# Last three tiles of a routed expert stage added through one-hot products instead of a scatter, with adds on GpSimd and stores on SyncE

## The reference, cut to what matters

```python
x = x + L0_ffn(L0_cond(x))      # attention-like pooling, then 8 dense experts of 512, gated by a k-th value
x = x + L1_ffn(L1_cond(x))      # adapter and layer norm, then the routed experts below
# L1_ffn(x):
xn = layernorm(x) * gamma + beta
probs = softmax(xn @ gate_w)                 # 8 experts
w, idx = top_k(probs, 2); w = w / sum(w)     # two experts for each token
h = gelu(xn @ w1[e] + b1[e]); out_e = h @ w2[e] + b2[e]
output = sum over the two experts of w * out_e
return output + x
```

## Time and profile before

| what | us |
|---|---|
| median of 3 runs | 396.54 (393.29 to 401.63) |
| profiled execution, time | 395.97 |
| profiled execution, span | 394.1 |
| granted TensorE clock, mean over the span | 0.926 |

### The profile page before, as it was taken

How to read it: one execution, slowest core, us unless ns; L and a number is a source line. 1 busy time by engine, 2 the same in 40 slices (tenths; PEclk the granted TensorE clock), 3 DMA queues, 4 the chain that set the end, 5 groups by cost and what they waited for, 6 DMA issues and landing times.

```text
span 394.1 us, 9605 instructions
## 1 busy us (share of the span) xinstructions
PE 338.7 (86%) x3422; PEld 243.9 (62%) x3422; DVE 282.7 (72%) x779; ACT 250.0 (63%) x345; POOL 101.9 (26%) x97
## 2 busy tenths in 40 slices
PE   8999999888999999999979969699886934889930
PEld 5657776666777666767756646477664713567720
DVE  1746589999999978798977999735666422546684
ACT  3368588677998887998887758455653503346520
POOL 0000000000000000122227575404345372526770
PEclk9897999999999999999999989799986885999995
DMA  6993003022443674500001012211211012121354
GB/s 189 291 373 107 2 0 98 25 70 58 124 151 130 228 245 173 220 2 2 2 0 42 16 49 59 71 23 41 63 27 55 16 54 69 39 57 55 116 148 141
DMA packets 27059, 35.80 MB, mean 91 GB/s; under 512 B 6581, under 2 KB 22853, under 8 KB 26789
## 3 DMA queue, kind: packets, MB, share of 16 engines
q1 hardware_dynamic: 21600, 28.40, 23.1%
q0 software_dynamic: 2400, 4.95, 3.8%
q10 hardware_dynamic: 3012, 1.84, 1.5%
HBM read 29.18 MB, written 16.25 MB: 115 GB/s over the span
## 4 chain that ended last, share of the span: by engine, by line
PE 61%; DVE 16%; issue 8%; ACT 6%; another core or an unknown queue 5%; DMA 2%; POOL 1%; ACTq 0%; DVEq 0%; SPq 0%; POOLq 0%
PE bank L663 5%; DVE l L710 5%; PE psA L616 5%; PE psA L617 5%; PE psA L618 5%; PE bank L665 5%; PE bank L664 5%; PE bank L653 4%; PE psA L601 4%; PE psA L597 3%; PE psA L603 3%; PE psA L602 2%; PE bank L654 2%; PE bank L1068 2%
## 5 line engine op out<-in xcount | busy, mean ns | idle before, releaser
L710 DVE SCALAR_TENSOR_TENSOR l<-h 128x1024 f16<-128x1024 f32 (+1 forms) x90 | 104.7, 1165 | 15.3 <-ACT h L703 15.0
L663 PE MATMUL bank<-w,h 128*128 128x128 f16 x512 | 91.2, 221 | 3.4 <-issue 2.1
L689 ACT ACTIVATE h<-psA,b1f 128x512 f32<-128x512 f32 (+1 forms) x100 | 76.7, 800 | 25.6 <-PE psA L618 21.9
L703 ACT ACTIVATE h<-h 128x1024 f16<-128x1024 f32 (+1 forms) x90 | 91.0, 1011 | 1.4
L665 PE MATMUL bank<-w,l 128*128 128x128 f16 x512 | 91.2, 221 | 0.0
L664 PE MATMUL bank<-w,h 128*128 128x128 f16 x512 | 91.1, 221 | 0.0
L1816 POOL DMA_INDIRECT sorted_out<-w,xe x43 | 50.3, 1169 | 49.0 <-DVE w L1865 23.3
L684 ACT ACTIVATE h<-psA 128x1024 f32<-128x1024 f32 (+1 forms) x22 | 22.1, 1004 | 59.9 <-PE psA L603 42.6
L663 PEld LDWEIGHTS bank<-w,h 128*128 128x128 f16 x512 | 50.5, 99 | 13.9 <-issue 6.0
L1404 POOL TENSOR_SCALAR rs<-mv 128x4 f32<-128x4 f32 x8 | 4.0, 498 | 200.3 <-DVE mv L1385 199.9
L664 PEld LDWEIGHTS bank<-w,h 128*128 128x128 f16 x512 | 50.5, 99 | 5.6
(11 more groups left out here) (214 smaller groups left out, 574.3 us busy)
## 6 DMA issues: line engine op xcount, KB each, us to landing
sorted_in<-in_pad SPq DMA_DIRECT2D x14, 715.0 KB, 7.1
w<-in_w SPq DMA_DIRECT2D x8, 512.0 KB, 5.6
wraw<-in_w SPq DMA_DIRECT2D x8, 512.0 KB, 3.8
first<-sorted_in SPq DMA_DIRECT2D x43, 65.0 KB
w<-sorted_out SPq DMA_DIRECT2D x6, 256.0 KB, 3.9
mg<-in_maskt SPq DMA_DIRECT2D x8, 128.5 KB, 3.5
acc<-in_xtm SPq DMA_DIRECT2D x2, 512.0 KB, 5.5
mg<-in_gbc SPq DMA_DIRECT2D x8, 128.0 KB
```

Source lines behind the costliest of these rows:

```text
L663: pe.matmul(oo, a, w_h, start=(c == 0 and k == 0), stop=False, skip_group_check=True)
L689: last = act.activation(dst[:, q * w:q * w + w], src[:, q * w:q * w + w], ACT.Gelu_apprx_tanh, bias=b1f[:, es[q] * 4 + c:es[q] * 4 + c + 1 ...
L703: act.activation(wide(h16, h16_at[u], u), wide(h32, h32_at[u], u), ACT.Copy, scale=HS).then_inc(s_hi, 1)
L710: dve.scalar_tensor_tensor(wide(l16, h16_at[u], u), wide(h32, h32_at[u], u), HS, wide(h16, h16_at[u], u), ALU.mult, ALU.subtract).then_inc ...
```

## The change

It does six things.

- `HOTP = 2`: the last two pairs, tiles 40 to 42 (`HOT` = 3), are not scattered. For each of their rows the weight of its choice is computed on the spot: the row carries a third word, the difference of the two best router values (`ROW` = D + 3), ScalarE takes its tanh (`act_ht`), VectorE makes the weight (`dve_hw`) and then a 128x512 matrix with that weight where the row's token number equals the column's (`dve_hot`, against `iota`, the numbers of group 3's tokens). TensorE multiplies it with `yo` in fp32 (`pe_hot`, four products of 128x128x128 for a tile) and gathers all three tiles in one PSUM bank; VectorE adds it to group 3 in two halves (`add_hot`). As not every row of group 3 is now written in `sorted_out`, both its parts are zeroed early (`zero_rows`).
- `last_load` waits for tiles 0 to 39 alone.
- `POOL_GROUPS = (0,)`: group 0's results are weighed and added on GpSimd, in four operations on 128x512 (`pool_adds`). The adds of groups 1 and 2 stay on VectorE, in steps of two.
- The stores of groups 0 to 2 move from ScalarE's queue to SyncE's, behind SyncE's own `last_load`, in the order 2, 1, 0.
- The turned copies of pairs 13 to 21 move from VectorE to ScalarE.
- Many numbers of MID, PRO, AT, TILE, SPACE, BP, W0HI and W0LO are changed by small amounts.

```diff
-ROW = D + 2
+ROW = D + 3
+HOTP = 2
+POOL_GROUPS = (0,)
...
+HOT = 1 + 2 * (HOTP - 1) if TPB[-1] % 2 else 2 * HOTP
...
-TILE = [1.35, 1.26, 1.27]
+TILE = [1.35, 1.29, 1.28]
...
-     "top": 18, "tanh": 17.4, "wk": 29, "rk": 19.7, "rkd": 21.7, "sc": 21.7, "gd": 32, "gT": 35.8, "gTc": 35.4, "b2m": 35.8,
+     "acc": 15.6, "top": 18.4, "tanh": 17.4, "wk": 26.7, "rk": 20.1, "rkd": 20.7, "sc": 19.1, "gd": 31.2, "gT": 33.5,
...
-      "out": 3.2, "in": 9.3, "b2": 3.2, "moe0": 3.5, "moe1": 12.6, "moeg": 3.6, "moek": 1.8, "yg": -5.5, "ygs": 0.7,
-      "tab": 0.45}
+      "out": 3.2, "in": 9.3, "b2": 3.2, "moe0": 0.4, "moe1": 12.6, "moeg": 3.45, "moek": 1.6, "yg": -9, "ygs": 0.4,
+      "tab": 0.45, "hots": -5, "hot": 2.5, "pm": 3, "pms": 1.05}
...
+            if g == NG - 1:
+                terms.extend((MO[g] + AT["moek"] * h, "moe", (g, h)) for h in range(2))
+            elif g not in POOL_GROUPS:
+                terms.extend((MO[g] + AT["moeg"] * (g - len(POOL_GROUPS)) + AT["moek"] * (k + 0.5 * h), "moe", (g, k, h)) for k in range(2) for h in range(2))
+        for h in range(2):
+            terms.append((MO[NG - 1] - AT["moek"] + 0.5 * h, "hot", (NG - 1, h)))
...
+        def add_hot(i, v):
...
+                dve.wait_ge(t_hot, 1)
+                o = bank[mb[("hot", 0)][0]].rearrange("p (t d) -> p t d", t=4)[:, 2 * h:2 * h + 2, :]
+                a = acc[:, 4 * g + 2 * h:4 * g + 2 * h + 2, 0:D]
+                dve.tensor_tensor(a, a, o, ALU.add).then_inc(s_acc, 1)
...
+        def zero_rows(sp):
+            for k in range(2):
+                sp.dma_start(scy[k * N + N - 512:k * N + N, :], t["zero"]).then_inc(t_pad, 16)
...
-            at("pool", m2_pos(u, last) + AT["out"], pool_out)
+            if i < NTL - HOT:
+                at("pool", m2_pos(u, last) + AT["out"], pool_out)
...
+            def act_ht(act):
...
+                act.activation(hth[:, h0:h1].unsqueeze(2), xrf[:, tiles[0]:tiles[-1] + 1, D + 2:D + 3], ACT.Tanh, scale=0.5).then_inc(t_ht, 1)
...
+            def dve_hw(dve):
...
+                link(dve, "dve", dve.tensor_tensor(hw[:, h0:h1], hsg[:, h0:h1], hth[:, h0:h1], ALU.mult))
+                link(dve, "dve", dve.tensor_scalar(hw[:, h0:h1], hw[:, h0:h1], c, c, ALU.mult, ALU.add))
...
+            def dve_hot(i):
...
+                    dve.tensor_scalar(hots[:, j, :], iota, xrf[:, i, D + 1:D + 2], hw[:, j:j + 1], ALU.is_equal, ALU.mult)\
+                        .then_inc(t_hp, 1)
...
+            def pe_hot(pe):
+                o = misc_bank(pe, ("hot", 0))
+                pe.wait_ge(t_yo, n + 1)
+                pe.wait_ge(t_hp, h1)
+                for i in tiles:
+                    j = i - (NTL - HOT)
+                    for x in range(4):
+                        last = pe.matmul(o[:, x * 128:x * 128 + 128], hots[:, j, x * 128:x * 128 + 128], yo[:, yo_at(i), :],
+                                         start=(j == 0 and x == 0), stop=(j == HOT - 1 and x == 3), skip_group_check=True)
...
+            if n >= NP - HOTP:
+                p = m2_pos(US + n, len(tiles) - 1) + AT["y"]
+                at("act", mpos[("t", n)] + AT["tc"] + 0.1, act_ht)
+                at("dve", mpos[("t", n)] + AT["xe"] + 0.7, dve_hw)
+                for i in tiles:
+                    at("dve", p + AT["hots"] + 0.5 * (i - tiles[0]), dve_hot(i))
+                at("pe", p + AT["hot"], pe_hot)
...
-            if b < NB - 1:
-                at("act", mpos[("t", n)] + AT["tc"], act_x)
-            else:
-                at("dve", mpos[("t", n)] + AT["tc"], dve_x)
+            at("act", mpos[("t", n)] + AT["tc"], act_x)
...
-                scattered(eng, NTL)
+                scattered(eng, NTL - HOT)
...
+        def pool_adds(g, n):
...
+                w = wk[:, g, k, :].unsqueeze(2).to_broadcast([128, 4, D])
+                link(pool, "pool", pool.tensor_tensor(y, y, w, ALU.mult))
...
+                pool.tensor_tensor(group_acc(g), group_acc(g), y, ALU.add).then_inc(t_pm[g], 1)
...
-            at("act", 997 + 0.1 * g, store(g))
+            if g in POOL_GROUPS:
+                for n in range(4):
+                    at("pool", tpos(NTL - 1) + AT["pm"] + AT["pms"] * (4 * g + n), pool_adds(g, n))
+            at("sp", 998 + 0.1 * (NG - 1 - g), store(g))
         for h in range(2):
             q = ("sp", "act")[h]
-            at(q, 998 if h == 0 else 999, last_load(h))
+            at(q, 998, last_load(h))
             at(q, 1999, last_store(h))
```

More of the change, by code:

```diff
@@ L287, in build_adaln_ffn @@
         xa, x2, xn = (pro[:, n:n + 512].rearrange("p (t d) -> p t d", d=D) for n in (1024, 1536, 2048))
+        hots = pro[:, 0:HOT * 512].rearrange("p (t n) -> p t n", t=HOT)
+        iota = mg[:, 0:512]
         xsf = pro[:, 2560:2560 + 8 * ROW].rearrange("p (t d) -> p t d", t=8)
@@ L330, in build_adaln_ffn @@
         xk = sb("xk", [128, 2])
+        hsg, hth, hw = (sb(x, [128, HOT]) for x in ("hsg", "hth", "hw"))
         tei = sb("tei", [128, NB, 2, TPM], I32)
@@ L363, in build_adaln_ffn @@
         t_end = sem("t_end")
+        t_ht = sem("t_ht")
+        t_pm = [sem(f"t_pm{g}") for g in POOL_GROUPS]
+        t_hp = sem("t_hp")
+        t_hot = sem("t_hot")
         t_pad = sem("t_pad")
@@ L370, in build_adaln_ffn @@
         t_tr = sem("t_tr")
-        t_xt = [sem(f"t_xt{b}") for b in range(NB)]
+        t_xt = sem("t_xt")
         t_yo = sem("t_yo")
         t_so = [sem(f"t_so{i}") for i in range(NSO)]
-        t_yg = [sem(f"t_yg{i}") for i in range(NG * 2 + 2)]
+        t_yg = [sem(f"t_yg{i}") for i in range(NG + 1)]
         p_at = sem("p_at")
@@ L482, in group_of @@
         def group_of(kind, v):
-            return STEPS[v[1]][v[2]][1] if kind == "y" else (v[0] if kind == "moe" else v)
+            return STEPS[v[1]][v[2]][1] if kind == "y" else (v[0] if kind in ("moe", "hot") else v)
         b2_pos = [max(PG + 1.5 + KEPT * ND, 0) + 1.0 + AT["b2"] * g for g in range(NG)]
@@ L492, in build_adaln_ffn @@
             terms.append((mid_pos("b2x", g), "b2x", g))
-            for k in range(2):
-                terms.append((MO[g] + (AT["moeg"] * g if g < 3 else 0.0) + AT["moek"] * k, "moe", (g, k)))
+            if g == NG - 1:
[4 more added lines that the diff above has]
+            terms.append((MO[NG - 1] - AT["moek"] + 0.5 * h, "hot", (NG - 1, h)))
         terms.sort(key=lambda x: x[0])
@@ L521, in build_adaln_ffn @@
             misc.append((upos[US + n] - AT["t"], ("t", n), turned_at(n)))
+        misc.append((tpos(NTL - 1) + 3.0, ("hot", 0), None))
         misc.sort(key=lambda x: x[0])
@@ L742, in before @@
             g = group_of(terms[i][1], terms[i][2])
-            prior = [j for j in range(i) if group_of(terms[j][1], terms[j][2]) == g and terms[j][1:] != ("moe", (NG - 1, 0))]
+            other = [(k, (NG - 1, 1 - terms[i][2][1])) for k in ("moe", "hot")] if g == NG - 1 and terms[i][1] in ("moe", "hot") else []
+            prior = [j for j in range(i) if group_of(terms[j][1], terms[j][2]) == g and terms[j][1:] not in other]
             if prior:
@@ L810, in fn @@
                     return
-                for j in range(4):
+                for j in (2 * half, 2 * half + 1):
                     last = dve.scalar_tensor_tensor(acc_of(4 * g + j), yg[:, g, k, j, :], wk[:, g, k, j:j + 1],
@@ L815, in add_moe, with fn @@
             return fn
+        def add_hot(i, v):
+            g, h = v
+            def fn(dve):
+                before(dve, i)
+                dve.wait_ge(t_hot, 1)
+                o = bank[mb[("hot", 0)][0]].rearrange("p (t d) -> p t d", t=4)[:, 2 * h:2 * h + 2, :]
+                a = acc[:, 4 * g + 2 * h:4 * g + 2 * h + 2, 0:D]
+                dve.tensor_tensor(a, a, o, ALU.add).then_inc(s_acc, 1)
+            return fn
         for i, (pos, kind, v) in enumerate(terms):
-            make = {"y": gated, "b2": add_b2, "x2": add_x2, "b2x": add_b2x, "moe": add_moe}[kind]
+            make = {"hot": add_hot, "y": gated, "b2": add_b2, "x2": add_x2, "b2x": add_b2x, "moe": add_moe}[kind]
             at("dve", pos, make(i, v))
@@ L1878, in dve_xe @@
                                          xrf[:, i:i + k, D + 1:D + 2], ALU.mult, ALU.add).then_inc(t_xe, 1)
+                if n >= NP - HOTP:
+                    j = i - (NTL - HOT)
+                    link(dve, "dve", dve.tensor_scalar(hsg[:, j:j + k], xk[:, 0:k], 2.0, -1.0, ALU.mult, ALU.add))
+            h0 = tiles[0] - (NTL - HOT)
+            h1 = h0 + len(tiles)
+            def act_ht(act):
+                for i in tiles:
+                    act.wait_ge(t_xr[i % NX], 16 * (i // NX + 1))
+                act.activation(hth[:, h0:h1].unsqueeze(2), xrf[:, tiles[0]:tiles[-1] + 1, D + 2:D + 3], ACT.Tanh, scale=0.5).then_inc(t_ht, 1)
@@ new lines, in dve_hw, with fn @@
+            def dve_hw(dve):
+                c = 0.5 / (WS * HS)
+                dve.wait_ge(t_ht, n - (NP - HOTP) + 1)
+                link(dve, "dve", dve.tensor_tensor(hw[:, h0:h1], hsg[:, h0:h1], hth[:, h0:h1], ALU.mult))
```

(12 more changed lines are left out.)

59 lines of the change are left out of this document (41 added, 18 removed), and 46 rows, old and new, of tables (MID, PRO).

## The result

| what | before | after |
|---|---|---|
| median, same chip and session, 11 runs each | 394.90 us | 397.43 us |
| ratio to before, 95% interval | | 1.0092 [1.0046, 1.0137] |
| profiled execution, time | 395.97 | 397.19 |
| profiled execution, span | 394.1 | 395.4 |
| mean granted clock over the span | 0.926 | 0.929 |

The changed kernel is about 1% slower, where 393.5 was predicted against 396.54 (a ratio of 0.992). It lies inside the range given (up to 398.5), on the other side of no change.

What follows compares the result with a forecast made beforehand. TensorE's work bounds the last stage, a chain of handovers the end. Copies +0.7 and one-hots +0.95, then VectorE's 10.2 us list, end the span at 391.1 instead of 394.1: 393.5 us against the 396.54 median, range 387.5 to 398.5.

Steps and rivals of the forecast that it cites:

- So the next pair starts about 0.1 late, which eight pairs (14 to 21) make some 0.7: Last stage of tiles: turned copy behind ScalarE's activation delays each next pair about 0.1 us, some 0.7 in all.
- 8 × 0.47 = 3.8: Last stage: upper bound in us for the copies, if each of eight pairs pays ScalarE's full 0.47.
- fits in what TensorE still has to do: Pair 19: the one-hot's 0.4 us delay on VectorE is hidden under TensorE's remaining work, so costs nothing.
- rival C: Last stage: ScalarE's copy costs its full 0.47 per pair, 3.8 us instead of 0.7; time 396.6; chance 0.11.
- TensorE works at 100% there, which covers most of it: Last stage: argument against the copy costing its full 0.47 us per pair, as TensorE's full business hides most.
- A: End: rival that GpSimd's group 0 adds and VectorE's adds lock each other out, adding 2.2 us; time 395.7; chance 0.2.
- 20 adds beside scatters in 5.58: End: argument against the GpSimd lock, VectorE's adds beside GpSimd's scatters being no slower than 0.28 us each.
- 16.9 us were forecast: End: time from pair 20's activation to the span's end, with VectorE's list of 10.2 us as the bound.
- rival B: End: GpSimd's four ops at 2.6 us each finish last and delay SyncE's stores; time 400.9; chance 0.08.
- T + 4.4: Pair 20: its low part on VectorE ends 4.4 us after its activation starts, 0.95 later than before.
- The tables, costed at 0: Whole kernel: retiming by the moved positions was given no cost or gain, with a range of ±3 us.
- rival D: Before 328 us: moved positions shorten the 14.6 us hole, a third of it giving 4.9 us more; chance 0.18.

Runs made afterwards that it cites:

- e2: Changed kernel with group 0's adds back on VectorE instead of GpSimd, copies still on ScalarE: median 396.26 us, 1.0047 of before.
- e1: Changed kernel with the turned copies of pairs 13 to 21 back on VectorE, all else as changed: median 392.93 us, 0.9927 of before.
- e4: Kernel before with only the turned copies of pairs 13 to 21 moved to ScalarE: median 401.04 us, 1.0158 of before.
- e7: Changed kernel with copies and group 0's adds on VectorE and the old number tables except AT: median 375.29 us, 0.9862 of before.
- e10: Changed kernel with copies and group 0's adds on VectorE, new tables, run again beside the changed kernel: median 393.40 us, 0.9951 of before.

## Why the prediction was wrong, and where it held

**The step that failed: "So the next pair starts about 0.1 late, which eight pairs (14 to 21) make some 0.7".** The mechanism was looked at, and the term sized too small: 0.7 us where it measured 3.7 (stage 32.63 with the copies on ScalarE, 28.96 with them on VectorE). In a turn, the start moved by 0.19 (from + 1.46 to + 1.65), not 0.1, and the first products, which I left as they were, take 0.16 longer (2.43 from the first bias to the next activation instead of 3.73 − 1.46 = 2.27). With the batch's last steps that is 1.7 us. The other 2.0 lie in the batch's first two steps, which I counted like any other: some 0.5 is the later copy at the full clock (7.72 in `e2`), the rest goes with the clock, granted at 0.81 over these steps in both profiled executions of the changed kernel. I had no term for that. In the kernel before, the copy alone made the stage 5.3 us longer, 3.5 of it in these two steps with the clock at 0.68. My upper bound, 8 × 0.47 = 3.8, just held in the changed kernel and not there, since I priced the copy by what it adds to ScalarE's list and not by what it does to a ring of two engines. The one-hots took another 0.44 of the stage, where my "fits in what TensorE still has to do" gave them nothing ahead of pair 20. The argument against rival C, "TensorE works at 100% there, which covers most of it", is the reading that misled me: 24.00 of 24.00 us is a modelled busy time of overlapping products and leaves no room to see how long the ring activation, copy, first products is. After the change it still reads 23.73 of 24.00 with 8% fewer products. The Trainium skill (Perfetto Trace Analysis, "Identifying the Most-Contended Engine") warns that TensorE's busy share is no good measure of how close a kernel is to its limit, since its instructions are pipelined, and points to the share of the peak arithmetic rate and to the weight loads' busy share instead; here the weight loads fall from 18.58 to 17.91 us in the same stretch, and the record count from 295 to 272, as a turn of 4.1 us in place of 3.73 would have it.

**Rivals A and C came together.** C (0.11), the copy at 3.8 us, is what the stage shows at 3.7. A had a chance of 0.2 at 2.2 us. Each had a chance as the only one, and both at once had none. C alone is enough to put the kernel behind the one before: with A undone it is at 1.005 (`e2`), with C undone at 0.993 (`e1`). Beside GpSimd's four operations, two adds took 2.15 instead of 0.61 and four took 3.28 instead of 1.14 (both values from the same places in the run with both parts undone, 1.14 there): 3.7 us. GpSimd's operations, at 1.06 to 1.18, gained 8 adds for VectorE, 2.5 us, and cost it 3.7. The net 1.2 is what undoing it brought from pair 20 to the end (19.5 to 18.3, 19.1 to 17.9). My argument against it, 20 adds beside scatters in 5.58, was one about scatters: a scatter does not slow VectorE's adds, GpSimd's arithmetic does. The Trainium skill (SBUF — State Buffer, "Who interferes with whom") says that a VectorE instruction with two SBUF inputs contends with a GpSimd instruction that reads SBUF, over a shared port pair that one of them holds exclusively; the trace agrees, with VectorE as the loser at 2.15 and 3.28 us.

**What held.** The end's own gain. From pair 20's activation 16.9 us were forecast (391.1 − 373.5 − 0.7) against 20.6 before. Without the two costs it is 17.9, with 2.5 us of group 0's adds back on VectorE; with GpSimd's help it is 19.5, with 3.7 us of the lock in it. Taking either away leaves 15.4 and 15.8: by these sums, which no run shows, the end alone was forecast a little too dear. Loads together at 383.99 and 384.01 (2 later than the 382 named, behind the longer stage), no scatter after tile 39, GpSimd at 1.2 at most, no rival B. Fp32 products at the full clock: 16 records in 2.02 us for my 2.2, 8 in 1.13 for my 1.1; they ended at 389.2 and not 385.5 because the sum ahead of them was held up by the adds. Low part 20 ended at T + 4.15 for my T + 4.4 (T is pair 20's activation; in the kernel before it is T + 3.43, not the T + 3.47 I wrote), with one-hots at 0.54 where I took 0.42 (0.69 was the bound). The tables, costed at 0, are worth −2.1 us on the chip where before takes 375.02. On the others, what the ratios leave after the traces' part from pair 13 on has no clear sign: for the changed kernel 3.6 to 4.5 us by the ratios, 2.5 of it in the traces; with both undone −4.0 to −1.9, −2.5 of it in the traces.

In sum, of +1.3 in the span: the part ahead of pair 13 gave −1.15, the stage +4.1 (3.7 the copies, for which 0.7 was forecast, and 0.4 the one-hots), the end −1.65 by the time from pair 21's activation (18.0 to 16.3). With copy and lock undone the kernel is at 0.990 and 0.995 of before, around the 0.992 that was predicted for all of it.

**Open.** Why the first products lengthen by 0.1 a half when they start just behind the copy: the gaps are between single products and no wait is named for them. It goes with the copy's place, as the early transposes take it away, but nothing here separates its cause. Why the clock fell at the start of the batch in the changed kernel (0.81, with the old tables too), in `e4` (0.68) and in `e7` (0.67) and not in `e2` (1.00), where TensorE had waited as long for the copy: no run shows it. And the hole, below.

## What to carry to other kernels

An instruction moved to an idle engine is priced by what stands ahead of it there, not by its length: 0.59 us of copy behind an activation cost a loop 0.35 us in each turn, and ahead of the activation nothing. Where such a move lets TensorE wait longer, look at the granted clock behind the wait too: here the lower clock followed in four of the five profiled executions with the copy in that place, and cost more than the wait. Follow the ring of waits around a loop and measure its time by the distance of two equal instructions, not by TensorE's busy share. And before adds are shared between VectorE and GpSimd, count what each loses beside the other: here a help of 2.5 us cost 3.7.

## What was unexpected of the hardware

The same kernel before takes 394.47, 393.56 and 394.90 us in three of the comparisons and 375.02 in the fourth, on another chip. A large part of the difference is a hole, a time in which TensorE and ScalarE stand still. The stretches of the kernel before with after's tables on that chip, where it is missing:

```profile
300.00:313.00 13.00, 12.19 (x130) 9.47 (x129) 9.12 (x45) 7.17 (x10) 6.01 (x6) 0.87 0.09 27
313.00:328.00 15.00, 12.97 (x140) 9.29 (x139) 7.72 (x15) 5.28 (x8) 11.54 (x12) 1.00 0.32 90
```

In 313 to 328 TensorE is busy for 12.97 us there. The stretches of the kernel before in its own comparison:

```profile
300.00:313.00 13.00, 12.03 (x100) 9.48 (x101) 7.33 (x39) 4.92 (x8) 3.01 (x4) 0.68 0.04 12
313.00:328.00 15.00, 5.54 (x52) 3.21 (x49) 3.56 (x15) 0.90 (x1) 10.35 (x11) 0.80 0.21 66
```

The hole in which ScalarE waits 14.60 us for nothing that is named is missing on the other chip. All four traces from that chip lack it, with the old tables and the new; all others have it, with waits of 9 to 15 us. So it goes with the chip, or with the time at which that chip was used, which no run separates, and the positions do not make it. My rival D, a hole shortened by the moved positions, came in form only: the longest wait of ScalarE fell from 14.60 to 9.97 us in the changed kernel, but another of 5.39 follows in it, and pair 13's activation was only 1.15 us earlier. The positions may shape it: the wait is 14.60 and 14.57 us in the two kernels with the old tables, and 9.0 to 11.4 in the eight with the new. The granted clock just ahead of it is lower too in the kernel before (0.68 against 0.87 over 300 to 313), but that is not its cause, since in `e10` it is 1.00 and the hole is there. Its cause is not settled, and the difference between the chips is some five times as large as the effect that was studied here.
